# New instruction lists for the first and last batches, for the loads and for the rounds between them

## Time and profile before

| | |
|---|---|
| median of 3 runs | 568.94 us (567.25 to 571.3) |
| profiled execution | 569.02 us |
| its span | 567.4 us |
| PE, PEld busy | 468.3, 397.0 us |
| DVE, ACT, POOL busy | 325.0, 237.7, 231.2 us |
| mean granted clock | 0.943 |
| moved by DMA | 40.22 MB |

### The profile page before, as it was taken

The page is one execution under the profiler, slowest core; times in us unless marked ns, Lnnn a source line. Parts: engine busy times, 40 slices in busy tenths (PEclk is TensorE's granted clock), DMA queues, the critical chain, the costliest instruction groups (busy, mean ns, idle before and its releaser), DMA issues. The chain is left out here.

```text
span 567.4 us, 9625 instructions
## 1 busy us (share of the span) xinstructions
PE 468.3 (83%) x3644; PEld 397.0 (70%) x3644; DVE 325.0 (57%) x597; ACT 237.7 (42%) x465; POOL 231.2 (41%) x203
## 2 busy tenths in 40 slices
PE   0387773878799979998999899989998898699567
PEld 0266462756599858985898589858986796498366
DVE  0835676585685667566856686667664753461111
ACT  3115221125444553555355545454555346227222
POOL 0735167228324822482348233823382253211022
PEclk9996695599999999999999999999999999889879
DMA  8812202502801080109010901090009003600000
GB/s 281 301 43 74 88 1 92 94 2 72 186 1 63 10 205 2 57 16 204 2 49 25 204 1 41 32 205 1 22 2 203 1 3 120 86 1 3 20 0 20
DMA packets 33276, 40.22 MB, mean 71 GB/s; under 512 B 3152, under 2 KB 28240, under 8 KB 32976
## 3 DMA queue, kind: packets, MB, share of 16 engines
q1 hardware_dynamic: 33232, 39.61, 27.1%
HBM read 28.85 MB, written 10.49 MB: 69 GB/s over the span
## 5 line engine op out<-in xcount | busy, mean ns | idle before, releaser
L1081 PE MATMUL ps<-splz,wh 128*128 128x256 f32 x512 | 98.9, 288 | 3.0 <-POOL splz L377 3.0
L942 DVE TENSOR_REDUCE nm<-ps 128x2 f32<-128x512 f32 x128 | 84.5, 688 | 17.8 <-PE ps L1277 16.7
L603 ACT ACTIVATE ya<-ps 128x512 f32<-128x512 f32 x128 | 72.0, 599 | 52.6 <-PE ps L1301 51.1
L377 POOL TENSOR_TENSOR hs<-g,hs 128x512 fp32r<-128x512 f32 x32 | 41.4, 1293 | 107.1 <-ACT hs L659 107.1
L1081 PEld LDWEIGHTS ps<-splz,wh 128*128 128x128 f32 x512 | 80.7, 194 | 5.5 <-issue 5.4
L1081 PE MATMUL ps<-splz,wl 128*128 128x256 f32 x256 | 72.9, 285 | 0.0
L1277 PE MATMUL ps<-kst,qst 96*128 96x256 f32 x256 | 52.8, 306 | 6.2 <-DVE nm L942 3.0
L1081 PE MATMUL ps<-wh,hs 128*128 128x256 f32 x256 | 55.8, 285 | 0.8 <-POOL hs L377 0.8
L1301 PE MATMUL ps<-qst,kst 100*128 100x256 f32 x256 | 53.5, 306 | 2.4 <-ACT ya L603 1.5
L649 ACT ACTIVATE g<-ps 128x512 f32<-128x512 f32 x32 | 19.2, 600 | 72.8 <-PE ps L1081 72.8
L1081 PEld LDWEIGHTS ps<-splz,wl 128*128 128x128 f32 x256 | 49.4, 193 | 0.0
(11 more groups left out here) (136 smaller groups left out, 970.7 us busy)
## 6 DMA issues: line engine op xcount, KB each, us to landing
qk_d<-ya SPq DMA_DIRECT2D x16, 512.0 KB, 2.8
qst<-qk_d SPq DMA_DIRECT2D x24, 256.0 KB, 5.1
kst<-qk_d SPq DMA_DIRECT2D x48, 128.0 KB, 5.9
adjD<-adj SPq DMA_DIRECT2D x8, 440.0 KB, 4.1
ya<-wall SPq DMA_DIRECT2D x12, 256.0 KB, 4.5
xT<-xt SPq DMA_DIRECT2D x8, 256.0 KB, 2.7
x_add<-x SPq DMA_DIRECT2D x8, 256.0 KB, 3.7
result<-xr SPq DMA_DIRECT2D x8, 256.0 KB, 3.1
```

The source lines that it names most:

```text
L377: pool.tensor_tensor(into, whole, high.bitcast(FP32), ALU.subtract).then_inc(signal.sem, 1)
L603: act.activation(ex[:, h % EXR], ps[:, h % 2].rearrange("p (c s) -> p c s", c=TC), ACT.Exp, scale=SCALE).then_inc(ex_ok.sem, 1)
L942: dve.tensor_reduce(nm[:, :, h], ps[:, h % 2].rearrange("p (c s) -> p c s", c=TC), AX.X, ALU.max, negate=True).then_inc(mx_ok.sem, 1)
L1081: ins = pe.matmul(dst, lhs(a, k), rhs(c, k), start=first_ and n == 0 and m == 0, stop=last_ and n == len(ks) - 1 and m == 2, **kw)
```

## The change

All five lists are written anew. `rounds` is gone; `program(head, round_, tail)` runs a written-out head (layer 0 of batches 0 to 2, q/k of 0 and 1, scores of 0), the round for `it` from 2 to 6, and a written-out tail (batches 5 to 7).

```diff
-        def rounds(round_):
-            for it in range(-3, B + 2):
-                round_(it)
+        def program(head, round_, tail):
+
+            head()
+            for it in range(2, 7):
+                round_(it)
+            tail()
```

```diff
+            def head():
+                load_xt(0)
+                weights("qk", 1)()
+                get_rope()
+                weights("self", 0)()
+                cond()
+                get_vec()
+                get_wb()
+                load_adj(0)
+                get_wkv()
+                get_angles()
+                weights("q0", 0)()
+                weights("q0", 1)()
+                weights("g", 0)()
+                get_consts()
+                weights("qk", 0)()
+                weights("g", 2)()
+                get_wc2()
+                weights("u", 3)()
...
```

```diff
-                    if b == 0:
-                        pe.wait_ge(qz_ok.sem, qz_ok.at(0))
-                    pe.wait_ge(nz_ok.sem, nz_ok.at(b))
-                    pe.matmul(ps[:, BANK["self"], o * S:(o + 1) * S], qz[:, o * P:(o + 1) * P], nzT[:], start=False, stop=True).then_inc(self_ps.sem, 1)
+                            lambda a, k: splx[:, a, k, :], range(KC)).then_inc(self_ps.sem, 1)
+            def qb(b):
...
+                    ins = act.activation(qbias[:, k, :], nzT[:], ident_fn, scale=qcol[:, k, b:b + 1], bias=vec[:, V_BSELF + k:V_BSELF + k + 1])
+            def selfadd(b):
...
+                dve.tensor_tensor(self32[:], ps[:, BANK["self"]].rearrange("p (k s) -> p k s", k=KC), qbias[:], ALU.add).then_inc(self_ok.sem, 1)
```

```diff
+            def klow(b):
+                dve.wait_ge(qkh_ok.sem, qkh_ok.at(b))
+                dve.wait_ge(qkT_ps.sem, qkT_ps.at(b))
+                dve.tensor_tensor(qkl[:, KC:2 * KC].bitcast(F32R), qk32[1], qkh[:, KC:2 * KC], ALU.subtract).then_inc(kl_ok.sem, 1)
```

```diff
+            def warm(i, bank, n):
+
+                def step():
+                    if i == 0:
+                        pe.wait_ge(onesr_ok.sem, onesr_ok.at(0))
+                    for _ in range(n):
+                        pe.matmul(ps[:, bank, 0:P], onesr[:], onesr[:], start=True, stop=True)
+                return step
```

**The lists.** TensorE's new head, from its start to the first scores:

```diff
+            def head():
+                warm(0, 2, 20)()
+                rsum(0)
+                cond_q()
+                warm(1, 2, 6)()
+                selfm(1)(0)
+                selfm(0)(0)
+                warm(2, 2, 6)()
+                kv0(0)
+                warm(3, 2, 9)()
+                q0(0, 1)(0)
+                kT(0)
+                q0(0, 0)(0)
...
+                x1T(0)
+                rsum(1)
+                warm(8, 2, 9)()
+                selfm(1)(1)
+                selfm(0)(1)
+                nxT(0)
+                kv0(1)
+                warm(9, 2, 7)()
+                kT(1)
+                qk(0)(0)
+                qk(1)(0)
...
+                v(0)(0)
+                pTt(1)(1)
+                warm(13, 2, 12)()
+                s(0)(0)
+                s(1)(0)
```

More of the change, by code:

```diff
@@ L351, in _ @@
-            rounds(round_)
+            def head():
[17 more added lines that the diff above has]
+                weights("u", 3)()
+                weights("g", 1)()
+                weights("g", 3)()
+                get_bo()
+                load_xt(1)
+                weights("u", 1)()
+                weights("u", 2)()
+                load_adj(1)
+                weights("u", 0)()
+                weights("o", 0)()
+                weights("v", 0)()
+                get_wc3()
+                load_x_add(0)
+                weights("d", 1)()
+                weights("d", 2)()
+                load_adj(2)
+                weights("d", 3)()
+                load_xt(2)
+                store_hi(0)
+                load_x_add(1)
+                weights("d", 0)()
+                store_lo(0)
+                stack(0)
+                nrows(0)
+                load_xt(3)
+                store_hi(1)
+                load_adj(3)
+                load_x_add(2)
+                store_lo(1)
+                stack(1)
+                nrows(1)
+                load_x_add(3)
+                load_xt(4)
@@ new lines, in round_, with tail @@
+            def round_(it):
+                step(load_adj, it + 2)
+                store_hi(it)
+                store(it - 2)
+                store_lo(it)
+                stack(it)
+                nrows(it)
+                step(load_x_add, it + 2)
+                step(load_xt, it + 3)
+            def tail():
+                store_hi(7)
+                store(5)
+                store_lo(7)
+                stack(7)
+                nrows(7)
+                store(6)
+                store(7)
@@ L352, in _ @@
+            program(head, round_, tail)
             sp.wait_ge(res_out.sem, 16 * B)
@@ new lines, in tail @@
+            def tail():
+                nxl(7)
+                hlow(3)(5)
+                radd0(7)
+                qlow(7)
+                x1bias(7)
+                rms2(6)
+                nzl(6)
+                hlow(0)(6)
+                hlow(1)(6)
+                hlow(2)(6)
+                hlow(3)(6)
+                rms2(7)
+                nzl(7)
+                hlow(0)(7)
+                hlow(1)(7)
+                hlow(2)(7)
+                hlow(3)(7)
+            program(head, round_, tail)
```

1345 lines of the change are left out of this document (960 added, 385 removed).

## The result

The changed kernel takes **544.91 us** (median of 4 runs, 543.15 to 546.69) against 568.10 (4 runs, 566.79 to 571.30): ratio 0.9584, 95% interval 0.9531 to 0.9637, faster. The forecast was 533 with a range of 516 to 551: direction and range held, the size did not. Of 36 us forecast, 23 came. The profiled execution has a span of 543.5 us (545.3 with what lies around it).

The account below looks back on a forecast made before the run. TensorE's in-order list was taken to bound the steady rounds, a serial chain through all engines the head and tail. From a span of 567.4 us, head -27, rounds -5 and tail -4, plus 1.6, gave 533; range 516 to 551.

Parts of the forecast that it names:

- The head, -27: Start up to the first row maxima: 30 us earlier, less 3 for hand-offs between engines; bounds -18 and -34.
- To x1: Head, from `am(0)` at about 26 to x1 added at 44.5: about 18.5 us, 20.5 earlier than before.
- From s(0) to the row maxima: End of head: s(0) starts at 74.5 at the earliest, batch 0's 16 maxima end at 95, VectorE near its limit.
- The engine trades: Steps moved between engines: VectorE +2 us per batch, ScalarE +1.8, covered by TensorE's list; 0.8 per moved step.
- The steady rounds, -0.8 for each of six: Rounds between head and tail: -5 us in all, bounds -12 and +6, limited by under 2 us of chain slack.
- the two places: Steady round: `pTt(0)` put before `pv(3)` and row sums before x1T fill TensorE waits with 0.4 and 0.47 us of work.
- The tail, -4: Last stretch: near 40 products at 0.117 instead of 0.21 us once products of ones fill waits; bounds 0 and -6.
- some behind 491.68: Tail: some products after the last batch's scores start, expected at 0.117 instead of 0.21 us, part of 3.8 us.
- VectorE: Rival: VectorE bounds the head and shows in rounds, four moved steps costing 0.8 more each; 548 us, chance 0.15.
- Transfers: Rival: loads queued behind a low-half store land 12 us late, so the head gains 15; 545 us, chance 0.07.
- The rounds recover more: Rival: steady rounds gain 2.5 us each and the head its 34; 516 us, chance 0.14.
- Slower, by products of ones on the path: Rival: 261 products in head and tail cost 0.22 us each, 57 in all, none covered; 590 us, chance 0.04.

Follow-up runs that it names:

- experiment 4: Changed kernel with `cond_2(1)`, 16 products, moved from ahead of `y(0)` to where 14 products of ones stood; 542.05 us, ratio 0.9516 to the kernel before.
- experiment 7: As experiment 4, with VectorE's two casts of ones also moved behind the adjacency passes of batch 1; 543.89 us, ratio 0.9544 to the kernel before.
- experiment 9: Changed kernel with twice the products of ones in the tail (194 instead of 97); 548.46 us, ratio 0.9630 to the kernel before.
- experiment 8: As experiment 7, with batch 2's adjacency passes moved behind the row maxima of batch 0; 546.58 us, ratio 0.9593 to the kernel before.
- experiment 1: Changed kernel without any of its 261 products of ones; 550.58 us, ratio 0.9674 to the kernel before.
- experiment 2: Changed kernel without the head's 164 products of ones, keeping the tail's 97; 547.20 us, ratio 0.9600 to the kernel before.
- experiment 10: Changed kernel with 20 instead of 8 products of ones in the head's wait for `yadd(1)`; 543.11 us, ratio 0.9559 to the kernel before.
- experiment 5: Changed kernel with `aadd`, the sum of affinities and bias, back on GpSimd in all batches; 552.31 us, ratio 0.9702 to the kernel before.
- experiment 11: As experiment 4, with `cond_2(0)` behind `y(0)` and the casts of ones behind `yadd(0)` and `klow(0)`; 545.24 us, ratio 0.9548 to the kernel before.
- experiment 3: Changed kernel with the first 21 loads in the kernel before's order, first input sixteenth; 556.00 us, ratio 0.9761 to the kernel before.
- experiment 6: Changed kernel with `pTt(0)` behind `pv(3)` and the row sums behind x1T again in steady rounds; 546.46 us, ratio 0.9582 to the kernel before.
- experiment 12: Kernel before with only `aadd` moved to VectorE, right behind `am`, in all eight batches; 571.06 us, ratio 1.0035 to the kernel before.

## Why the prediction held in its range, and which of its steps failed

**The head, -27: measured -18.7.** Its early half was right to within a microsecond (row sums, self, `am(0)`), and so was its next link, x1 to the store: 15.66 us, forecast 15.6 (as a sum; its terms weren't compared one by one). Its clock was mixed: the products of `self` still stand 0.21 apart (12.23 to 15), those of q0 from 19.17 on 0.12.

The step that failed is "*To x1* ... about 18.5": it took 25.5. It counted VectorE, GpSimd and the two function tables on ScalarE, and forgot TensorE's own queue: `cond_2(1)` ahead of `y(0)`, 3.4 us, of which experiment 4 recovered 2.15. The rest is in the lines shown, priced from them and not by an experiment of its own: `y(0)` at half clock (1.7); GpSimd's first product 1.0 longer (experiment 7: `y(0)` 0.96 earlier without that); `cond_2(0)` ahead of the second transposes (0.8, from the end of GpSimd's second product at 38.57 to 39.38); `nz(1)` ahead of `x1add(0)` (up to 0.9). The price of `cond_2` could be read before: 32 such products had 6.8 us in the page of the kernel before.

The low half left 2.1 us behind the high one, where the forecast had 0.8 (74.5 less 60 and 13.7), and the 13.7 was 14.26. So the terms missed by 6.2, 0, 1.3, 0.6 and, for the next one, 3.2: 11.3, of which the 3 us for hand-offs that I took off had covered a part, and 8.3 are left. The load of x_add(0), forecast to land at 44, was issued at 44.35 and landed 2.7 us later; x1 was late enough that it held nothing.

From s(0) to the row maxima 20.5 were forecast and 23.7 measured, with the TensorE products behind `yadd(1)` 0.21 apart. The same lists took 20.7 in experiment 9 with the products at 0.12 (timelines of TensorE, of the kernel after and of experiment 9):

```profile
93.92 0.76 PE L1491 MATMUL ps<-splx,wh 128*128 128x256 f32 x2 [0.21 <-DVE x L1122]
```
```profile
92.43 0.47 PE L1491 MATMUL ps<-splx,wh 128*128 128x256 f32 x2 [0.40 <-DVE x L1122]
```

The busy windows of that stretch, of the kernel after and of experiment 9 (the clock is the third number from the end):

```profile
82.73:106.41 23.68, 19.18 (x116) 15.14 (x116) 19.29 (x34) 4.33 (x11) 7.35 (x8) 0.78 0.00 1
```
```profile
81.93:102.59 20.66, 16.82 (x118) 13.53 (x119) 18.48 (x35) 4.21 (x11) 8.73 (x8) 0.93 0.00 1
```

So about 3 us of the missing 8 are the clock of one execution, and the first row maxima of one list leave anywhere from 102.6 to 106.4. Over the other kernels (experiment 8 aside, whose VectorE list differs there) it is much the same: 20.4 to 20.7 us at 0.92 (experiments 1, 2, 4 and 7), 21.1 at 0.88 (10), 22.8 at 0.85 (5), 23.6 at 0.78 (11), 25.2 at 0.73 (3); experiment 6 is off that line with 21.9 at 0.78. Experiments 1 and 2 have no products of ones in the head, so it isn't these that keep the clock there. What decides it stays open.

**The engine trades, at nothing in the rounds: undoing one of them, `aadd`, cost 0.7 to 0.95 a round.** The duration was well bounded: `aadd` 0.892 us in the mean (taken 0.8), `klow` 1.249, the rotation sum 0.692 (groups by line):

```profile
L1082 DVE TENSOR_TENSOR aff<-aff,off 128x640 f32<-128x640 f32 x16 | 14.3, 892 | 0.1
L1173 DVE TENSOR_TENSOR ya<-k,ya 128x512 fp32r<-128x512 f32 x8 | 10.0, 1249 | 0.7 <-ACT ya L660 0.7
L1157 DVE TENSOR_TENSOR ya<-ya 128x512 f32<-128x512 f32 x8 | 5.5, 692 | 0.3
```

In the head `aadd(0)` took 0.82 and `aadd(1)` 1.26 beside GpSimd's subtraction (timelines of VectorE and of GpSimd):

```profile
28.54 1.26 DVE L1082 TENSOR_TENSOR aff<-aff,off 128x640 f32<-128x640 f32 x1
```
```profile
27.86 1.27 POOL L423 TENSOR_TENSOR aff<-aff,amx 128x640 f32<-128x640 f32 x1 [9.98 <-DVE amx L1089]
```

By the Trainium skill (SBUF — State Buffer, the section on the two separate sides) the two exclude each other, and the one that starts first holds the other out for its whole instruction. The trace agrees: when `aadd(1)` came, 0.59 us of the subtraction were left, and it took 0.44 longer. The forecast's 2.1 by that page was for two steps that start together, which these don't. What the forecast missed is the other side of the trade. It asked what VectorE pays and called GpSimd "not the bound"; but the sum also lay on a chain, and with a shorter step on it (0.8 for 1.56) the new lists can be tighter; how the longer step comes to delay the exponentials that TensorE waited for in experiment 5 wasn't followed. Experiments 5 and 12 together show an interaction: the new lists, at least with the sum in the place tried, need the trade, and the trade is worth nothing without the lists. The other trades weren't tried.

**The steady rounds, -0.8 for each of six: measured -1.03 for four, and +0.62 in sum over the other three intervals.** The size is near, the account was wrong: of the 1.1 named, the two places gave 0.25 instead of 0.87, for the reason in experiment 6. The two products (0.23) weren't tried alone, and about 0.55 of the round is left, which the other changes of order or the engine trades must have brought; which of them stays open.

**The tail, -4: measured -1.7.** The mechanism held. The twelve products behind the wait of 1.93 run at 0.12 now and give 1.2, as priced. Behind the wait of 3.01 not ten but some fifteen had run at half clock (544.27 to 547.4), and they give 1.5. By experiment 1 the products of ones are worth 3.1 us in the last stretch (58.84 less 55.75). What the forecast put at nothing is the rest of the written-out tail: without products of ones it took 58.84 us at a mean clock of 0.88, against 57.46 at 0.91 before, 1.4 longer; whether by its order or by the clock stays open. The "some behind 491.68" made up the other 1.8 of the forecast and gave nothing: behind s(0) of the last batch the products are still 0.21 apart in the kernel after, from 473.14 to 479, and that stretch took 51.02 instead of 50.79. The wait of 2.37 for the transfer of the last scores stays, with 24 products of ones in it and 0.65 left.

**The rivals.** *VectorE* (548): its signs didn't appear (`aadd` and `radd1` are below 1.3; the last maximum of batch 0 ends at 104.94, just under the 105 named), and experiment 5 speaks against it; experiment 8 doesn't decide. *Transfers* (545) hit the time by luck, not the cause: x1 was added 6.2 us later than forecast, but its row in VectorE's timeline shows no wait for a transfer. *The rounds recover more*: no; they gave some 1.03 each. *Slower, by products of ones on the path*: its turning point, 0.16 us each uncovered, was never near, since in the tail each group leaves a wait behind it; but experiment 9 shows the price, 5.9 us for 97 or 0.06 each, half of it covered. And in experiment 10 the unchanged tail shows it in small (timeline of TensorE):

```profile
518.96 4.51 PE L1536 MATMUL ps<-onesr 128*128 128x128 f32 x20
523.27 0.73 PE L1491 MATMUL ps<-splz,wh 128*128 128x256 f32 x2
```

The same 20 took 2.43 us in the kernel after with 0.82 of wait behind them; here they ran at half clock, ended late, and this last stretch was 58.50 us.

## What to carry to other kernels

When a chain is summed over several engines, go through each engine's list once more and ask what stands *ahead* of each link; the largest forgotten term here was 16 tiny products on the engine that seemed to be idle. Before moving work into a wait, look what that work itself waits for: shared banks and buffers tie it to the very event that it should bridge. An engine trade and an order of the lists can be worth something only together, so undoing one of them measures the pair and not the part. An experiment in which the clock can differ needs the clock of its stretch beside it: here the same instructions took 20.7 or 23.7 us, as much as most of the edits are worth.

## What the runs showed of the hardware

The granted clock of a list is not a constant of it. Ten kernels (after, and experiments 2 to 8, 10 and 11) have the same lists in the last stretch: seven took 55.74 to 55.84 us for it, three 57.29, 57.46 and 58.50 (experiments 2, 6 and 10). Windows of the last one, experiment 10, show where: 0.74 of the full clock, with TensorE busy throughout, where the kernel after had 1.00. Just before, at 518, both had waited the same 0.89 us.

```profile
510.00:520.00 10.00, 8.01 (x62) 7.72 (x62) 2.58 (x6) 2.40 (x8) 0.88 (x2) 0.92 0.00 0
520.00:530.00 10.00, 10.00 (x66) 10.00 (x66) 1.12 (x2) 3.36 (x5) 1.37 (x2) 0.74 0.01 2
```

The Trainium skill (TensorE: Matmul & The Clock Gate, the section on the clock gate) has activity lift the throttle. The products of ones agree with it on the whole (experiment 1, 5.7 us), and this stretch shows that a busy engine can still be at 1.2 GHz for a while.

A GpSimd product beside a VectorE cast of 4x2048 elements, only four partitions wide, went from 1.27 to 2.26 us: the cast is tiny in data and costs its neighbour 1 us. It runs from 31.80 to 33.09 and the product ends at 34.23, about as if it had begun when the cast ended. Without the cast beside it (experiment 7) the same product takes 1.27.
